# The output stored by GpSimd's indirect transfers, one tile at a time, in place of SyncE's plain ones

## Chip, cores and metric

The kernel runs on one core of one Trainium2 chip. The metric is the device time in microseconds of one execution. Engines are named as in the profile: PE (TensorE), DVE (VectorE), ACT (ScalarE), POOL (GpSimd), SP (SyncE).

## What is computed

Four transformer layers in sequence, each a cross-attention and a feed-forward part, on x of 16 x 256 rows of 128 float32 values (4096 rows) with a context of 16 x 64 rows. The parts are called a0, f0, a1, f1, a2, f2, a3, f3. The last, f3, is a mixture of 8 experts of which the best two count for each row, with 2 shared experts that always count:

```python
p = softmax(h @ gate_w.T)                        # h: x normalised
gate = where(p + gate_bias >= second largest, p, 0)
x = x + sum(gate[e] * (silu(h @ w1[e].T) * (h @ w3[e].T)) @ w2[e].T for e in range(8))
x = x + (silu(h @ sw1.T) * (h @ sw3.T)) @ sw2.T
```

The output is x after f3, 4096 rows of 128 float32, 2.1 MB.

## The kernel before

The state stays on the chip for the whole program, in the buffer X of 128 partitions by 32 tiles by 128 values: row 128 t + p of the output is partition p of tile t. The work goes by groups of four tiles (GT = 4), 8 groups (N_GROUPS), in every part. All engines run their own program and wait for each other by semaphores.

In f3 each group goes through 10 chunks (CH3): 8 experts and 2 halves of the shared one. For a chunk PE makes two products of the turned rows with the weights (L2199 and L2202), ACT applies silu to the first (L2249), DVE multiplies with the second (L2270), and PE makes the product back to 128 columns (L2216 for experts, L2219 for the shared halves). DVE adds each expert's product, weighted by its gate, to X, tile by tile (L2279). After the last chunk DVE has, in this order: the gates of the next group (L2160 to L2181), the normalised rows of the group after it (L271), and the add of the shared part, L2297, which is the last write to a group's four tiles of X. It waits for that write and raises the semaphore `sem("f3", "res")` by one. So the result of a group is announced after L2297; DVE goes on with L2270 of the next group.

SP issues all loads at the start (L2357 to L2373; only the weights of f3 wait for space). Then it loops over the groups: it waits for a group's result (L2375), and stores the four tiles in one transfer of 256 KB (L2376), 512 pieces of 512 bytes. After the loop it waits until the eight have landed (`S("stored")`).

POOL, in f0, takes part in a reduction across partitions (L1174). In the attention parts it makes products for the values (L422) and adds bias rows to X (L415); in f2 it has most of its work (L1951, L1961). Its last work is that of attention a3, `heads_pool(pool, heads["a3"])`, the last call in its program. It has none in f3.

PE's program has its next groups' turned rows prepared ahead; the order of all engines in f3 is written out by hand.

Of the kernel before, what the change touches and what calls it, by code (L numbers as in the profile page):

```python
# [19 lines left out]
U8 = mybir.dt.uint8  # L20
I16 = mybir.dt.int16
U16 = mybir.dt.uint16
ALU = mybir.AluOpType
ACT = mybir.ActivationFunctionType
AX = mybir.AxisListType
ds = bass.ds

P = 128
B, SQ, SK, D = 16, 256, 64, 128
N_TILES = B * SQ // P  # L30
N_GROUPS = N_TILES // 4
GT = 4
# [39 lines left out]
def build(nc, dram):  # L72
    with ExitStack() as ctx:
        def sb(name, shape, dt=F32):
            return ctx.enter_context(nc.sbuf_tensor(name, shape, dt))
# [3 lines left out]
        def S(name):  # L79
            if name not in sems:  # L80
                sems[name] = ctx.enter_context(nc.semaphore(name))
            return sems[name]

        X = sb("X", [P, N_TILES, D])
# [10 lines left out]
        for k, parts in PACKS.items():  # L96
            pack_sb[k] = shared[k] if k in shared else sb("w_" + k, [P, WIDTH[k]])
            at = 0
# [55 lines left out]
        def groups2(eng, body):  # L154

            with eng.Fori(0, N_GROUPS // 2 - 1) as k:
                for j in range(2):
# [15 lines left out]
                   res=N_GROUPS, bn=N_TILES)  # L173
# [11 lines left out]
        def sem(s, name):  # L185
            return S("all_" + name)

        def at(s, name):
            return sum(count(x, name) for x in SUB[:SUB.index(s)])
# [18 lines left out]
        def ln_var_dve(dve, s, k=0):  # L208
# [7 lines left out]
            dve.wait_ge(sem(s, "stats"), at(s, "stats") + k + 1)  # L216
            dve.tensor_tensor(diff, me, mo, ALU.subtract).then_inc(ln, 1)
            dve.scalar_tensor_tensor(out=var, in0=ve, scalar=D * LN_EPS, in1=vo, op0=ALU.add, op1=ALU.add).then_inc(ln, 1)
            dve.tensor_tensor(mn, me, mo, ALU.add).then_inc(ln, 1)
            dve.wait_ge(ln, n + 1)  # L220
            dve.scalar_tensor_tensor(out=sq, in0=diff, scalar=0.25, in1=diff, op0=ALU.mult, op1=ALU.mult).then_inc(ln, 1)
            dve.wait_ge(ln, n + 3)
            dve.tensor_scalar(mn, mn, 0.5, None, ALU.mult).then_inc(ln, 1)
            dve.wait_ge(ln, n + 4)
            dve.scalar_tensor_tensor(out=var, in0=var, scalar=1.0 / D, in1=sq, op0=ALU.mult, op1=ALU.add)\
                .then_inc(sem(s, "var"), 1)
# [123 lines left out]
        def hs(name):  # L350
            return S("att_" + name)

        def hat(s, name):
            rotated = 2 if s == "a3" and name == "k_ps" else 0
            return ATT_A0.get(name, 0) + HSUB.index(s) * PER[name] + rotated
# [49 lines left out]
        def heads_pool(pool, L):  # L405
            s = L.s
            pool.wait_ge(S("rows"), 1)
            row = addrow[:, HAS_ROW[s], :]
            if s == "a3":
                pool.wait_ge(S("f2_tr"), 4 * N_GROUPS)  # L410

            def rows(g):
                pool.wait_ge(sem(s, "normed"), at(s, "normed") + g + 1)
                xg = X[:, ds(4 * g, 4), :]
                pool.tensor_tensor(xg, xg, row.unsqueeze(1).to_broadcast([P, GT, P]), ALU.add)\  # L415
                    .then_inc(sem(s, "biased"), 1)

            def weights(b):
                pool.wait_ge(hs("v"), hat(s, "v") + b // 4 + 1)
                if b >= 2:  # L420
                    pool.wait_ge(hs("pv"), hat(s, "pv") + b - 1)
                pool.tensor_tensor(  # L422
                    L.vw[b % 2].rearrange("p (q e n) -> p q e n", q=4, e=2),
                    tile_of(L.V2, b).rearrange("p (q n) -> p q n", q=4).unsqueeze(2).to_broadcast([P, 4, 2, 32]),
                    W["vmask8"].rearrange("p (e n) -> p e n", e=2).unsqueeze(1).to_broadcast([P, 4, 2, 32]),
                    ALU.mult).then_inc(hs("kv"), 1)

            def rotate(b):
                pool.wait_ge(S("att_qe"), b + 1)
                pool.tensor_tensor(L.qe[b % 2], L.qe[b % 2], W["cosq"], ALU.mult).then_inc(hs("r"), 1)  # L430
                pool.tensor_tensor(L.qse[b % 2], L.qse[b % 2], W["sinq"], ALU.mult).then_inc(hs("r"), 1)
                if b >= L.ahead:
                    pool.wait_ge(hs("st_ps"), hat(s, "st_ps") + b - L.ahead + 1)
                pool.wait_ge(hs("r"), 2 * b + 2)
                pool.tensor_tensor(L.qT[b % L.ahead], L.qe[b % 2], L.qse[b % 2], ALU.add).then_inc(hs("qT"), 1)

            if L.rope:
                rotate(0)
                rotate(1)
                weights(0)  # L440
                rotate(2)
                weights(1)
                rotate(3)
                rows(0)
                for b in range(B):
                    if b + 4 < B:
                        rotate(b + 4)
                    if b + 2 < B:
                        weights(b + 2)
                    if b % 2 and b // 2 + 1 < N_GROUPS:  # L450
                        rows(b // 2 + 1)
            else:
                for g in range(N_GROUPS):
                    weights(2 * g)
                    weights(2 * g + 1)
                    rows(g)
# [729 lines left out]
        gate_l = [levels(0), levels(1)]  # L1186
        sig_l = [levels(2, U16), levels(3, U16)]
        sig_f = [tmp_all[:, 2 * F0N + i * F0N:3 * F0N + i * F0N] for i in range(2)]
# [935 lines left out]
        f3 = Carve()  # L2124
# [177 lines left out]
            groups2(dve, body)  # L2302

        def setup_dve(dve):
            dve.wait_ge(S("ld_const"), 16)
            dve.memset(qs[:, 14:32], 0.0).then_inc(S("cst"), 1)
            dve.memset(qs[:, 13:14], ROUND).then_inc(S("cst"), 1)
            dve.tensor_copy(ident16[:, :], ident).then_inc(S("cst"), 1)
            dve.wait_ge(S("ld_x"), 16)  # L2310
            for t in range(LN0):
                dve.bn_stats(stats[:, t, :], X[:, t, :]).then_inc(S("bn0"), 1)
            dve.wait_ge(S("bn0"), LN0)
            dve.sem_inc(sem("a0", "stats"), 1)
# [39 lines left out]
        @block.sync  # L2354
        def _(sp):
            x_in = dram["x"].rearrange("(t p) d -> p t d", p=P)
            sp.dma_start(X[:, 0:LN0, :], x_in[:, 0:LN0, :]).then_inc(S("ld_x"), 16)  # L2357
            sp.dma_start(pack_sb["const"][:, :], dram["pack_const"]).then_inc(S("ld_const"), 16)
            sp.dma_start(pack_sb["a0"][:, :], dram["pack_a0"]).then_inc(S("ld_a0"), 16)
            sp.dma_start(ctx_sb[:, :, :].rearrange("p b k -> p (b k)"), dram["ctx"]).then_inc(S("ld_ctx"), 16)  # L2360
            sp.dma_start(mask_u8[:, :], dram["mask"]).then_inc(S("ld_mask"), 16)
            sp.dma_start(X[:, LN0:N_TILES, :], x_in[:, LN0:N_TILES, :]).then_inc(S("ld_x"), 16)
            sp.dma_start(kmrow_u8[:, :], dram["kmrow"].to_broadcast([P, B * SK])).then_inc(S("ld_kmask"), 16)
            sp.dma_start(kmT_u8[:, :], dram["kmT"]).then_inc(S("ld_kmask"), 16)
            sp.dma_start(pack_sb["f0"][:, :], dram["pack_f0"]).then_inc(S("ld_f0"), 16)
            sp.dma_start(rows_bc[:, :], dram["rows"].to_broadcast([P, 4 * P])).then_inc(S("ld_rows"), 16)
            sp.dma_start(gbias3[:, :], dram["gbias"].to_broadcast([P, E3])).then_inc(S("ld_rows"), 16)
            sp.dma_start(rscale[:, :], dram["rscale"].to_broadcast([P, 1])).then_inc(S("ld_rows"), 16)
            sp.dma_start(pack_sb["once"][:, :], dram["pack_once"]).then_inc(S("ld_once"), 16)
            for k in ("a1", "f1", "a2", "f2", "a3", "f3"):  # L2370
                if k == "f3":
                    sp.wait_ge(S("f0_o_ps"), N_GROUPS)
                sp.dma_start(pack_sb[k][:, :], dram["pack_" + k]).then_inc(S("ld_" + k), 16)  # L2373
            with sp.Fori(0, N_GROUPS) as g:
                sp.wait_ge(sem("f3", "res"), at("f3", "res") + g + 1 + 1)  # L2375
                sp.dma_start(dram["out"].rearrange("(g t p) d -> p g t d", p=P, t=GT)[:, ds(g, 1)]  # L2376
                             .rearrange("p a t d -> p (a t) d"), X[:, ds(4 * g, 4), :]).then_inc(S("stored"), 16)
            sp.wait_ge(S("stored"), 16 * N_GROUPS)

        @block.vector  # L2380
        def _(dve):
# [45 lines left out]
        @block.gpsimd  # L2427
        def _(pool):
            pool.wait_ge(S("ld_const"), 16)
            att0_pool(pool)  # L2430
            f0_pool(pool)
            heads_pool(pool, heads["a1"])
            heads_pool(pool, heads["a2"])
            f2_pool(pool)
            heads_pool(pool, heads["a3"])

def constants():
# [100 lines left out]
```

## Time and profile before

| | us |
|---|---|
| median of 3 runs | 1238.36 |
| lowest and highest run | 1228.98, 1240.29 |
| the profiled execution, by the same clock | 1236.59 |
| its span, from the first instruction to the last | 1234.8 |

The profile's page tells the busy time of each engine as a share of the span. The table of stretches tells the same for parts of it. A timeline lists instructions in order of time, merged where several of one line follow each other; behind each, in brackets, stands how long its engine sat idle before it and what it was released by. Transfers are issued by a queue (SPq); the time of an issue is not that of the transfer, which is told apart as time to landing. TensorE's granted clock is a share of full speed (2.4 GHz).

### The profile page before, as it was taken

What the parts mean: (1) busy time and instruction counts of PE and PEld (TensorE: products, weight loads), DVE (VectorE), ACT (ScalarE), POOL (GpSimd) and SP (SyncE); (2) the same over time, 40 slices, a digit from 0 to 9 for tenths busy, and PEclk for the clock granted to TensorE, in tenths of its full rate; (3) what the DMA queues carried; (4) which work ended last, traced back from release to release, by engine and by line L of the source; (5) the groups of instructions that cost most, each with busy time, mean ns of one, the idle gap of its engine ahead of it and who ended that gap; (6) DMA issues with size and microseconds to landing.
All of it is one profiled execution on the core that took longest, in us unless ns stands there. A gap on an engine that the chain in (4) does not pass through costs nothing.

```text
span 1234.8 us, 21182 instructions
## 1 busy us (share of the span) xinstructions
PE 1019.8 (83%) x7331; PEld 656.3 (53%) x7331; DVE 906.6 (73%) x2297; ACT 634.7 (51%) x1007; POOL 354.4 (29%) x334
## 2 busy tenths in 40 slices
PE   5868800679978997899669999998889979999998
PEld 3653300655546674454326667666645546666665
DVE  4685699858885674577678898999568876666666
ACT  3424578856632244565267777775466533333332
POOL 5600000002110003345098999995112200000000
PEclk9988965779999997999759999999989999999999
DMA  7000000010000000000000000000000000000000
GB/s 272 1 1 1 1 0 0 1 65 2 1 2 1 1 1 1 2 1 2 1 0 1 1 0 0 0 1 1 1 1 2 2 1 10 9 8 8 8 9 18
DMA packets 8959, 13.51 MB, mean 11 GB/s; under 512 B 816, under 2 KB 6704, under 8 KB 8624
## 3 DMA queue, kind: packets, MB, share of 16 engines
q1 hardware_dynamic: 8880, 12.46, 2.9%
q8 instruction: 50, 0.82, 0.3%
q14 instruction: 29, 0.24, 0.1%
HBM read 10.36 MB, written 2.10 MB: 10 GB/s over the span
## 4 chain that ended last, share of the span: by engine, by line
PE 43%; DVE 26%; issue 7%; ACT 4%; DVEq 0%; ACTq 0%
DVE big L785 7%; DVE hq L780 7%; PE psum L558 5%; PE psum L2216 5%; PE psum L2199 5%; PE psum L2202 5%; PE psum L1518 2%; DVE big L2041 2%; PE psum L1762 2%; PE psum L1770 2%; PE psum L512 2%; DVE big L789 2%; ACT psum L1879 2%; PE psum L1777 2%; PE psum L1773 2%
## 5 line engine op out<-in xcount | busy, mean ns | idle before, releaser
L780 DVE TENSOR_REDUCE hq<-psum 128x16 f32<-128x1024 f32 x96 | 114.3, 1221 | 82.7 <-PE psum L512 42.8
L1951 POOL TENSOR_TENSOR big<-big 128x512 f32<-128x512 f32 x128 | 128.6, 1043 | 21.4 <-ACT big L1856 21.4
L2249 ACT ACTIVATE big<-psum 128x512 f32<-128x512 f32 x80 | 47.7, 598 | 141.1 <-PE psum L2199 141.0
L422 POOL TENSOR_TENSOR big<-big,w_const 128x256 f32<-128x256 f32 x48 | 35.8, 748 | 260.3 <-PE psum L558 227.3
L1879 ACT ACTIVATE psum<-big,tmp 128x512 f32<-128x512 f32 x128 | 85.0, 687 | 25.0 <-DVE big L2041 22.3
L2041 DVE SCALAR_TENSOR_TENSOR big<-big,tmp,psum 128x512 f32<-128x512 f32 x128 | 90.4, 744 | 4.8 <-ACT psum L1879 1.9
L2270 DVE TENSOR_TENSOR big<-big,psum 128x512 f32<-128x512 f32 x80 | 54.4, 687 | 51.1 <-PE psum L2202 49.7
L668 ACT ACTIVATE big<-psum 128x1024 f32<-128x1024 f32 x64 | 62.0, 1021 | 55.1 <-PE psum L542 55.1
L785 DVE RECIPROCAL big<-psum 128x256 f32<-128x256 f32 x48 | 84.0, 1750 | 7.7 <-PE psum L558 7.6
L2216 PEld LDWEIGHTS psum<-tmp,big 128*128 128x128 f32 x512 | 66.7, 192 | 41.5 <-issue 38.0
L2279 DVE SCALAR_TENSOR_TENSOR X<-psum,big,X 128x128 f32 (+1 forms) x256 | 72.3, 344 | 17.9 <-PE psum L2216 15.5
L2202 PE MATMUL psum<-hT,tmp 128*128 128x512 f32 x160 | 81.8, 593 | 2.7 <-DVEq L2260 2.7
L1961 POOL TENSOR_TENSOR big<-big 128x1024 f32<-128x1024 f32 x32 | 75.2, 2360 | 26.3 <-DVE big L2041 26.3
L2199 PE MATMUL psum<-hT,tmp 128*128 128x512 f32 x160 | 82.5, 597 | 0.0
L1432 PE MATMUL psum<-f_downT,tmp 128*128 128x128 f32 x192 | 25.8, 301 | 68.0 <-DVE tmp L1315 68.0
L287 ACT ACTIVATE hT<-psum 128x512 f32<-128x512 f32 x64 | 38.1, 595 | 76.8 <-PE psum L282 76.8
L558 PE MATMUL psum<-big 128*32 128x256 f32 x768 | 53.1, 393 | 28.2 <-DVE big L789 28.2
L2216 PE MATMUL psum<-tmp,big 128*128 128x128 f32 x512 | 68.2, 276 | 8.5 <-DVE big L2270 8.5
L1201 DVE TENSOR_REDUCE amax<-big 128x1 f32<-128x1536 f32 x32 | 55.9, 1749 | 22.6 <-ACT big L1341 22.6
L282 PE MATMUL psum<-w_const,hrow 128*128 128x128 f32 x256 | 44.4, 301 | 33.8 <-DVE hrow L1225 10.9
L538 PE MATMUL psum<-hq,big 32*128 32x256 f32 x768 | 65.6, 428 | 6.9 <-DVE hq L780 6.6
L1801 PEld LDWEIGHTS psum<-w_const,big 128*128 128x128 f32 x512 | 61.0, 192 | 8.6 <-issue 8.6
(243 smaller groups left out, 2353.5 us busy)
## 6 DMA issues: line engine op xcount, KB each, us to landing
out<-X SPq DMA_DIRECT2D x8, 256.0 KB, 2.3
tmp<-in_pack_f SPq DMA_DIRECT2D x1, 1924.0 KB, 7.4
w_f<-in_pack_f SPq DMA_DIRECT2D x1, 1280.0 KB, 12.2
tmp<-in_pack_once SPq DMA_DIRECT2D x1, 960.0 KB, 7.1
X<-in_x SPq DMA_DIRECT2D x1, 768.0 KB, 5.3
w_a<-in_pack_a SPq DMA_DIRECT2D x3, 256.0 KB, 7.5
w_a<-in_pack_a SPq DMA_DIRECT2D x1, 704.0 KB, 9.6
w_f<-in_pack_f SPq DMA_DIRECT2D x1, 576.0 KB, 5.0
```

The costliest lines, as they stand in the source:

```text
L538: pe.matmul(bank(1 + r)[:, 256 * e:256 * e + 256], L.kbd[rows, b, e * P:(e + 1) * P], L.qT[b % L.ahead][rows, :], start=True, stop=False)
L558: ins = pe.matmul(bank(6)[32 * r:32 * r + 32, 256 * which:256 * which + 256], w, L.pt[b % 2][:, (2 * r + e) * 256:(2 * r + e + 1) * 256], ...
L780: dve.tensor_reduce(nm, psum[:, 1 + 2 * t:3 + 2 * t, :].rearrange("p c (r l k) -> p (c r) l k", r=2, k=SK), AX.X, ALU.max, negate=True).th ...
L785: dve.reciprocal(L.rz, bank(6)[:, 256:512]).then_inc(hs("rz"), 1)
L1879: act.activation(bank(EX_BANK + h % 2), ssum[t][:, h * 512:(h + 1) * 512], ACT.Exp, bias=shift2[:, t * NH2 + h:t * NH2 + h + 1]).then_inc( ...
L1951: ins = pool.tensor_tensor(ssum[t][:, h * 512:(h + 1) * 512].rearrange("p (i j) -> p i j", i=ROWS2), st[:, 0, h, 0:ROWS2].unsqueeze(2).to_ ...
L1961: pool.tensor_tensor(ew[t][:, 0:left], ew[t][:, 0:left], ew[t][:, NFOLD * 512:], ALU.add)\
L2041: dve.scalar_tensor_tensor(out=ew[t][:, blk], in0=ssum[t][:, blk], scalar=best2[:, t, h, 7:8], in1=bank(EX_BANK + h % 2), op0=ALU.is_ge, o ...
L2199: pe.matmul(bank(1 + e % 2), W["f3_w1"][:, e * P:(e + 1) * P], hT[:, j, :], start=True, stop=True)\
L2202: pe.matmul(bank(3 + e % 2), W["f3_w3"][:, e * P:(e + 1) * P], hT[:, j, :], start=True, stop=True)\
L2216: ins = pe.matmul(bk[:, t * P:(t + 1) * P], hid3[e % 2][:, t * P:(t + 1) * P], W["f3_w2"][:, e * P:(e + 1) * P], start=True, stop=True) \
L2279: dve.scalar_tensor_tensor(out=xt, in0=bank(5 + e % 2)[:, t * P:(t + 1) * P], scalar=gate3[:, t * E3 + e:t * E3 + e + 1], in1=xt, op0=ALU. ...
```

## The change

SP's loop over the groups, with its eight stores and the wait for them, is taken out. POOL gets a new function, `store_pool`, called behind `heads_pool(pool, heads["a3"])`. It writes a table of row numbers once: `tok_row[p, t] = 128 t + p`, 128 partitions by 32 unsigned integers. Then, for each group, it waits for the same semaphore value as SP did, and issues four indirect transfers, one for each tile: each takes its 128 row numbers from a column of the table and writes 128 rows of 512 bytes to the output. There are 32 in all, of 64 KB. At the end POOL waits for all of them. No other engine's program is changed.

```diff
@@ -2302,6 +2303,19 @@
             groups2(dve, body)
 
 
+        tok_row = sb("tok_row", [P, N_TILES], U32)
+
+        def store_pool(pool):
+
+            pool.iota(tok_row[:, :], [[P, N_TILES]], base=0, channel_multiplier=1).then_inc(S("tok_row"), 1)
+            pool.wait_ge(S("tok_row"), 1)
+            for g in range(N_GROUPS):
+                pool.wait_ge(sem("f3", "res"), at("f3", "res") + g + 1 + 1)
+                for t in range(4 * g, 4 * g + 4):
+                    pool.indirect_dma_start(dram["out"], bass.IndirectOffsetOnAxis(tok_row[:, t:t + 1], 0),
+                                            X[:, t, :], None).then_inc(S("stored"), 16)
+            pool.wait_ge(S("stored"), 16 * N_TILES)
+
         def setup_dve(dve):
             dve.wait_ge(S("ld_const"), 16)
             dve.memset(qs[:, 14:32], 0.0).then_inc(S("cst"), 1)
@@ -2371,11 +2385,6 @@
                 if k == "f3":
                     sp.wait_ge(S("f0_o_ps"), N_GROUPS)
                 sp.dma_start(pack_sb[k][:, :], dram["pack_" + k]).then_inc(S("ld_" + k), 16)
-            with sp.Fori(0, N_GROUPS) as g:
-                sp.wait_ge(sem("f3", "res"), at("f3", "res") + g + 1 + 1)
-                sp.dma_start(dram["out"].rearrange("(g t p) d -> p g t d", p=P, t=GT)[:, ds(g, 1)]
-                             .rearrange("p a t d -> p (a t) d"), X[:, ds(4 * g, 4), :]).then_inc(S("stored"), 16)
-            sp.wait_ge(S("stored"), 16 * N_GROUPS)
 
         @block.vector
         def _(dve):
@@ -2433,6 +2442,7 @@
             heads_pool(pool, heads["a2"])
             f2_pool(pool)
             heads_pool(pool, heads["a3"])
+            store_pool(pool)
```

## Rows read from the trace of the kernel before

**Rows 1.** The page: busy us (share of the span) xinstructions; the chain that ended last.

```profile
PE 1019.8 (83%) x7331; PEld 656.3 (53%) x7331; DVE 906.6 (73%) x2297; ACT 634.7 (51%) x1007; POOL 354.4 (29%) x334
...
PE 43%; DVE 26%; issue 7%; ACT 4%; DVEq 0%; ACTq 0%
```

**Rows 2.** Stretches of f3: length; busy us (xinstructions) by engine; clock, DMA share, GB/s.

```profile
1007.00:1033.00 26.00, 26.00 (x124) 16.68 (x122) 17.63 (x57) 9.09 (x14) 0.00 (x0) 1.00 0.00 1
...
1158.00:1182.00 24.00, 22.87 (x110) 14.72 (x109) 15.98 (x51) 8.17 (x12) 0.00 (x0) 1.00 0.04 11
...
1207.00:1232.00 25.00, 24.13 (x115) 15.45 (x113) 16.56 (x43) 5.38 (x9) 0.00 (x0) 1.00 0.04 11
```

**Rows 3.** Timeline of one expert in the last group: start us, us, instruction.

```profile
1220.28 1.02 PE L2202 MATMUL psum<-hT,tmp 128*128 128x512 f32 x2
...
1221.40 0.69 DVE L2270 TENSOR_TENSOR big<-big,psum 128x512 f32<-128x512 f32 x1 [0.65 <-PE psum L2202]
...
1222.23 1.13 DVE L2279 SCALAR_TENSOR_TENSOR X<-psum,big,X 128x128 f32<-128x128 f32 x4
...
1222.89 1.02 PE L2202 MATMUL psum<-hT,tmp 128*128 128x512 f32 x2
```

**Rows 4.** Timeline of the border between the first two groups of f3.

```profile
1031.70 1.16 DVE L271 TENSOR_SCALAR hrow<-X,lnw 128x128 f32 x4 [0.39 <-DVE big L2181]
...
1032.77 0.68 DVE L2297 TENSOR_TENSOR X<-X,psum 128x512 f32 x1
...
1033.78 1.28 DVE L2270 TENSOR_TENSOR big<-big,psum 128x512 f32<-128x512 f32 x2 [0.32 <-PE psum L2202]
...
1034.60 1.15 PE L2216 MATMUL psum<-tmp,big 128*128 128x128 f32 x8 [1.09 <-DVE big L2270]
```

**Rows 5.** Timeline of the last stores, and the end's instructions (duration ns, first and last start).

```profile
1207.02 25.47 SPq L2376 DMA_DIRECT2D out<-X  x2
...
1231.17 0.69 DVE L2297 TENSOR_TENSOR X<-X,psum 128x512 f32<-128x512 f32 x1 [1.25 <-PE psum L2219]
1232.11 0.38 SPq L2376 DMA_DIRECT2D out<-X  x1
...
L73 SPq COMPARE_BRANCH  x1: 38/38/38, 1234.4 to 1234.4; - x1
...
L73 PEldq EVENT_SEMAPHORE  x1: 51/51/51, 1234.8 to 1234.8; - x1
```

**Rows 6.** The stores' line: duration ns min/median/max, first and last start; time to landing.

```profile
L2376 SPq DMA_DIRECT2D out<-X x8: 378/378/415, 1033.7 to 1232.1; - x8
...
DMA to landing us min/median/max: 2.3/2.3/2.4
```

**Rows 7.** Waits of SP's queue: us in total, times, longest us.

```profile
SPq L2376 <- DVEq L2300: 969.5, 8, 777.5
...
SPq L73 <- DMA out<-X: 1.8, 1, 1.8
```

**Rows 8.** POOL's own lines: duration ns min/median/max, and its last work.

```profile
L422 POOL TENSOR_TENSOR big<-big,w_const x48: 722/725/1707, 229.2 to 986.5; 128x256 f32<-128x256 f32 x48
...
L415 POOL TENSOR_TENSOR X<-X,addrow x24: 1261/1266/1278, 246.3 to 987.2; 128x512 f32<-128x512 f32 x24
...
L1961 POOL TENSOR_TENSOR big<-big x32: 2342/2360/2375, 635.4 to 854.6; 128x1024 f32<-128x1024 f32 x32
...
987.17 1.26 POOL L415 TENSOR_TENSOR X<-X,addrow 128x512 f32<-128x512 f32 x1
```

**Rows 9.** POOL after its last reduction across partitions: timeline, and the queue's change.

```profile
221.69 0.37 POOL L1174 PARTITION_ALL_REDUCE qs<-qs  x1 [29.20 <-DVEq L1154]
229.18 1.42 POOL L422 TENSOR_TENSOR big<-big,w_const 128x256 f32<-128x256 f32 x2 [7.13 <-issue]
...
L422 POOLq MODIFY_POOL_CONFIG  x2: 85/85/85, 222.0 to 222.0; - x2
```

**Rows 10.** Timeline of SP's queue in the loads at the start: start us, us.

```profile
3.62 0.86 SPq L2362 DMA_DIRECT2D X<-in_x  x1
4.52 5.25 SPq L2363 DMA_DIRECT2D kmrow_u<-in_kmrow  x1
9.81 0.43 SPq L2364 DMA_DIRECT2D kmT_u<-in_kmT  x1
```

**Rows 11.** GB/s moved in 40 slices of 1230 to 1236 us.

```profile
GB/s 0 0 0 0 0 0 0 0 0 0 0 0 0 0 0 0 0 0 0 0 171 304 300 283 287 287 116 0 0 0 0 0 0 0 0 0 0 0 0 0
```

**Rows 12.** DVE's lines beside POOL's work and without it: duration ns min/median/max.

```profile
L2041 DVE SCALAR_TENSOR_TENSOR big<-big,tmp,psum x128: 735/743/750, 632.4 to 853.8; 128x512 f32<-128x512 f32 x128
...
L2270 DVE TENSOR_TENSOR big<-big,psum x80: 678/687/689, 1004.9 to 1229.2; 128x512 f32<-128x512 f32 x80
```

More of the change, by code:

```diff
@@ L22 @@
 U16 = mybir.dt.uint16
+U32 = mybir.dt.uint32
 ALU = mybir.AluOpType
```

## The prediction

> **What bounds the kernel now.** I read the page first for the shares of the engines [rows 1]. PE is busy for 83% of the span, DVE for 73%, POOL for 29%, and the chain that ended last is PE, then DVE. No share of it is a transfer. The change touches only the last stage, f3, so I then took the table by stretches of 24 to 26 us there [rows 2]. PE is busy for 23 to 26 us of each at full granted clock, DVE for 16 to 18, ACT for at most 9, and POOL does nothing: its column is empty from 1007 us on. The stage runs at the pace of PE. The reader is to see there that the engine that gets the new work is idle, and that the stores move only some 10 GB/s.
>
> Next I followed one expert in order of time [rows 3]. It repeats every 2.61 us (1220.28 to 1222.89), and DVE works 0.69 + 1.13 = 1.82 us of it, so DVE has 0.8 us to spare per expert. A group border is tighter [rows 4]: PE waits 1.09 us for the product of L2270 after the residual add L2297, and that row is the one place where a DVE delay reaches PE at once.
>
> Last I read the end [rows 5]. The last add, L2297, starts at 1231.17 and takes 0.69, so it ends at 1231.86. SP issues its last store at 1232.11, 0.25 us later. The store lands a median 2.3 us after its issue [rows 6], at 1234.4, where SP's last branch stands, and the last event is at 1234.8. **The tail that depends on how the output is written is thus 1234.8 - 1231.9 = 2.9 us**; all stores but the last land under the matmuls of a later group. The waits on SP's own queue say the same: it stood 969.5 us waiting for DVE in 8 waits, and 1.8 us waiting for a transfer, once [rows 7]. SP is never late.
>
> **The change, part by part.**
>
> *Removed:* eight issues of 256 KB on SP, 0.38 us each [rows 6]. Seven lie under PE's work and give back nothing. The eighth is in the tail. Its 2.3 us to landing is 0.38 of issue and 1.9 after it.
>
> *Added, the iota and its wait:* one 128x32 write on POOL. The nearest row is a 128x256 tensor operation on POOL at 0.72 us [rows 8]. POOL is free from 987.17 + 1.26 = 988.4 us, and the first group is ready only at 1033.7 [rows 6]. It costs nothing, with 45 us of cover; without that cover, under 1 us. POOL may also have to change its configuration for a kind of instruction that it has not run before. The trace shows one such change: after the fourth cross-partition reduction the next product, L422, starts 7.1 us late, with a change of POOL's configuration at its head and nothing else to wait for [rows 9]. Such a 7.1 us lies in the same 45, or, if it comes with the first scatter, under the 198 us between the first group and the last (1232.1 - 1033.7). In the tail it would cost 7.1 in full, but all scatters are of one kind, so it is over by then.
>
> *Moved:* the wait for a group's result goes from SP to POOL. It is moved past POOL's work of the attention stages, which is over at 988.4. Behind it on POOL stand only the later scatters and the last wait, and no engine waits for a semaphore of POOL in f3. On SP nothing is left behind the weight loads. The groups follow each other by (1232.1 - 1033.7) / 7 = 28.3 us on average, and the last two by 25.1 (the seventh store starts at 1207.0 [rows 5]). Four scatters fit in that as long as one takes less than 6.3 us. So 28 of the 32 scatters are hidden, and the last four are not.
>
> *Added, the last four scatters.* Each is an instruction on POOL that has to work out where 128 rows of 512 B go, 64 KB in all. The trace has no indirect transfer, and no transfer of POOL's. Call its time on POOL c. From below the nearest row is an SP issue, 0.38 us [rows 6], that is 1.5 us for four. From above it is POOL's slowest operation, 2.36 us (L1961) [rows 8], 9.4 for four; the slowest issue of a transfer on any queue is that of the mask row, 5.25 us [rows 10], 21 for four. I take the middle row of POOL, the 1.27 us of L415 [rows 8], because an instruction that handles each of 128 rows in software-like steps should cost more than the issue that SP makes in 0.38, and nothing in it touches as many elements as L1961 does. The four go one after another: 4 x 1.27 = 5.1 us. Then the last one has to land. I take the 1.9 us that the SP store needs after its issue. It may be 0.6 less, because only 64 KB are left and not 256 (the last store moved at close to 300 GB/s [rows 11], so 192 KB less is 0.6 us). The end after the landing stays 0.4 us.
>
> The sum, for the last group: 4c + 1.9 in place of 2.3, that is an addition of **4c - 0.4 us**. With c = 1.27 it is 5.1 - 0.4 = 4.7; with 0.38, 1.1 (0.5 with the faster landing); with 2.36, 9.0; with 5.25, 20.6. The profiled span becomes 1234.8 + 4.7 = 1239.5. That execution took 1236.59 us by the clock of the runs, which is 1.8 below the median of 1238.36, so on the median I forecast 1238.36 + 4.7 = **1243.1 us**.
>
> *What the transfers meet.* The 16 engines of DMA are idle in f3 but for the stores (a share of at most 0.04 in [rows 2]). Four transfers of 64 KB in place of one of 256 KB change nothing that anybody waits for before the end.
>
> *A rule that speaks against the change.* The last store's whole time to landing is 2.3 us in this trace, from SP [rows 6]. The Trainium skill (DMA: Bandwidth & Descriptors, Anatomy of one DMA — SWDGE (gpsimd) path) says that a transfer issued by GpSimd has a fixed cost of about 2.0 us plus its bytes by 436 GB/s, most of it the receipt from the memory written, and that descriptor generation is small. By that, an estimate from that page, four scatters overlap but for the issue and end 2.15 us after the last issue: an addition below mine. If they didn't overlap, four times 2.15 us would be 8.6, an addition of 6.3. Neither leaves 1%. No row here shows a transfer issued by POOL.
>
> **The rivals.** About 1% (12.4 us) is what a measurement of this kernel can tell from no change: its three runs alone spread over 11.3 us.
>
> *A. The tail grows by a few microseconds, the rest stays.* For it: POOL is empty, PE is the pace, the other 28 scatters have cover. Time 1239.5 to 1250, likeliest 1243. It holds for c up to 3.2 us, from 4c - 0.4 = 12.4.
>
> *B. One scatter costs much more than any operation of POOL here.* Its place is the same tail. It decides from c = 3.2 us. With c like the 5.25 of the mask row it gives 1238.4 + 20.6 = 1259. From 6.3 us on, the scatters of one group don't end before the next group, and the lateness adds up to the end. For it: that one SP issue [rows 10] shows that the making of a transfer can take that long. Against it: its neighbours take 0.86 and 0.43, and what it does, one short row into 128 partitions, is not what a scatter does.
>
> *C. POOL's work slows DVE at the borders of the groups.* The scatters of a group start right as DVE starts L2270 after L2297, and there PE already waits 1.09 us for DVE [rows 4]. If DVE stood still for all 5.1 us of each batch, at 7 borders, that would be 36 us, and 1243 + 36 = 1279. DVE gets back 0.8 us per expert, but PE has then already waited. It decides from (12.4 - 4.7) / 7 = 1.1 us lost per border. Against it: POOL writes little when it prepares a transfer. Where both worked at once in an earlier stage (L1961 from 635.4 to 854.6 in [rows 8]), this trace shows no cost to L2041, whose 128 rows keep between 735 and 750 ns for 128x512 beside 687 ns for L2270 without POOL [rows 12], at most 63 ns on each, and that is another operation. The Trainium skill (SBUF — State Buffer, Who interferes with whom) says that the two exclude each other where DVE runs in a 2-port mode or reads two inputs from SBUF. By that rule only L271, a tensor with scalars, could meet it, and at a border it ends before the result is announced; L2270 reads one input from PSUM. So by the rule C doesn't happen.
>
> *D. Nothing changes.* With c at 0.38 and the faster landing the addition is 0.5 us, 1239. The change does what it says, so the stores are certain to move; but the most that any other way to write the output could win is the 2.9 us of the tail, 0.2%. Faster by over 1% has no mechanism in this profile; I leave it only what the spread of the runs (1228.98 to 1240.29) could make.
>
> **How the numbers follow.** A 0.70, D 0.14, B 0.08, C 0.05, and 0.03 for a faster result from the spread alone. The time is that of A, 1243. The range: low 1233, which is D less the 6 us by which a median of this kernel may fall lower (its lowest run is 9.4 under the median). High 1256, which takes B in up to c = 4.5 us (4 x 4.5 - 0.4 = 17.6 above 1238.4) and leaves out its rest and C. Out of the range are then about 0.05 of C, 0.05 of B and 0.06 on either side for spread. Faster 0.03, within 1% 0.84 (A and D), slower 0.13 (B and C).
>
> **What the profile of the changed kernel would show.** POOL has 32 transfers in f3, in batches of four, each batch 25 us or more after the last one, and the time of one is c. The last L2297 still ends at about 1232 less or more the spread; from there to the end it is 7.6 us in place of 2.9. PE's wait at a border for L2270 stays near 1.1 us, which tells A from C. If the last scatter starts over 10 us after the last add, B is right. The prediction is wrong if c is above 3.2 us, if the transfers of one batch wait for each other's landing for more than 2 us each, if the end of the program after the last landing is no longer 0.4 us, or if L2270, or four of L2279, take longer than 0.69 and 1.13 us behind a batch.

## The result, and the profile after

The changed kernel takes 1244.62 us (median of 14 runs, 1236.90 to 1246.07), the kernel before 1238.14 (14 runs). The ratio is 1.0051 with a 95% interval of 1.0039 to 1.0063, that is 6.3 us more by the ratio (4.8 to 7.8): within 1%, and not zero. The profiled execution took 1244.06 us with a span of 1242.2. Lines of kernel.py are shifted: L2297 of before is L2298 now, L2270 is L2271, L2279 is L2280, L2216 is L2217, and the instructions that close the program, L73, are L74.

The page of the changed kernel (busy us, share of the span, instructions; the new line of POOL; the queue of POOL's transfers with packets, MB and share of 16 engines):

```profile
PE 1019.9 (82%) x7331; PEld 655.7 (53%) x7331; DVE 905.9 (73%) x2297; ACT 634.5 (51%) x1007; POOL 385.5 (31%) x367
...
q0 software_dynamic: 1024, 2.10, 0.5%
...
L2315 POOL DMA_INDIRECT out<-X,tok_row x32 | 31.0, 968 | 217.4 <-DVEq L2301 210.1
```

Against [rows 1] PE, DVE and ACT are unchanged. POOL has 31.1 us more work, and 31.0 of it are the 32 scatters. The span is 7.4 us longer, so the difference is a wait somewhere, and the end shows where. This is the timeline of the last 11 us, POOL and DVE among it:

```profile
1232.11 0.69 DVE L2298 TENSOR_TENSOR X<-X,psum 128x512 f32<-128x512 f32 x1 [1.25 <-PE psum L2220]
1233.13 0.95 POOL L2315 DMA_INDIRECT out<-X,tok_row  x1 [20.35 <-DVEq L2301]
1234.39 0.95 POOL L2315 DMA_INDIRECT out<-X,tok_row  x1 [0.30 <-issue]
1235.65 0.96 POOL L2315 DMA_INDIRECT out<-X,tok_row  x1 [0.30 <-issue]
1236.91 0.96 POOL L2315 DMA_INDIRECT out<-X,tok_row  x1 [0.30 <-issue]
```

and these are the instructions that close the program on POOL's queue and the last one of PE's (duration ns min/median/max, first and last start us), with the landing time of the scatters (its maximum of 3.3 belongs to the seventh group, not to the last).
```profile
DMA to landing us min/median/max: 2.2/2.2/3.3
```

```profile
L74 POOLq COMPARE_BRANCH  x1: 41/41/41, 1239.2 to 1239.2; - x1
L74 POOLq DRAIN  x1: 2682/2682/2682, 1239.3 to 1239.3; - x1
...
L74 PEldq EVENT_SEMAPHORE  x1: 51/51/51, 1242.2 to 1242.2; - x1
```

The last add ends at 1232.80. From there to the end it is now 9.4 us, where [rows 5] gave 2.9. The reader sees three pieces: 0.33 us until POOL starts and four scatters that start 1.26 us apart, to 1237.87; 1.3 us until the last one has landed, at 1239.2, where POOL's branch behind the wait stands; and then a DRAIN of POOL's queue that takes 2.68 us, so that 3.0 us pass from that branch to the end. In the kernel before, 0.4 us passed between SP's branch behind its wait and the end [rows 5]. The difference of the two tails, 9.4 - 2.9 = 6.5 us, is the whole of the measured 6.3. The last add itself ended 0.94 us later than in the kernel before (1232.80 and 1231.86). That is no effect of the stores: POOL's last addition, L416, ahead of all scatters, was already 0.97 us late (988.14, beside 987.17 in [rows 8]), and experiments 1 and 2 settle it.

At the borders of the groups nothing changed. The timeline of the first border, beside [rows 4]:

```profile
1033.72 0.68 DVE L2298 TENSOR_TENSOR X<-X,psum 128x512 f32 x1
1034.72 1.28 DVE L2271 TENSOR_TENSOR big<-big,psum 128x512 f32<-128x512 f32 x2 [0.32 <-PE psum L2203]
...
1035.55 1.15 PE L2217 MATMUL psum<-tmp,big 128*128 128x128 f32 x8 [1.09 <-DVE big L2271]
```

PE waits the same 1.09 us. The other borders agree: over all of f3, PE's waits for this product sum to 8.5 us in 7 times before and 8.4 us in 7 times after (the last column of the two pages):

```profile
L2216 PE MATMUL psum<-tmp,big 128*128 128x128 f32 x512 | 68.2, 276 | 8.5 <-DVE big L2270 8.5
...
L2217 PE MATMUL psum<-tmp,big 128*128 128x128 f32 x512 | 68.2, 276 | 8.4 <-DVE big L2271 8.4
```

All 80 of L2271 keep to the durations of [rows 12] within 1 ns, and here are also the 256 of L2280, after and before (there L2279):

```profile
L2271 DVE TENSOR_TENSOR big<-big,psum x80: 679/687/690, 1005.8 to 1230.2; 128x512 f32<-128x512 f32 x80
```

```profile
L2280 DVE SCALAR_TENSOR_TENSOR X<-psum,big,X x256: 339/343/352, 1007.9 to 1229.2; 128x128 f32 x96, 128x128 f32<-128x128 f32 x32
...
L2279 DVE SCALAR_TENSOR_TENSOR X<-psum,big,X x256: 339/343/352, 1006.9 to 1228.2; 128x128 f32 x96, 128x128 f32<-128x128 f32 x32
```

### The profile page after: what moved, and what is told of

Same layout as the page of the kernel before. It is cut to its first block, busy times and chain, and to the rows that moved or that the text cites. A ratio compares the mean times of both kernels' runs of the same rounds, so it can differ in the third digit from the quotient of the medians.

```text
span 1242.2 us, 21165 instructions
## 1 busy us (share of the span) xinstructions
PE 1019.9 (82%) x7331; PEld 655.7 (53%) x7331; DVE 905.9 (73%) x2297; ACT 634.5 (51%) x1007; POOL 385.5 (31%) x367
## 4 chain that ended last, share of the span: by engine, by line
PE 42%; DVE 26%; issue 7%; ACT 4%; DVEq 0%; POOL 0%; ACTq 0%
DVE hq L781 7%; DVE big L786 7%; PE psum L559 5%; PE psum L2217 5%; PE psum L2200 5%; PE psum L2203 5%; PE psum L1519 2%; DVE big L2042 2%; PE psum L1763 2%; PE psum L1771 2%; PE psum L513 2%; DVE big L790 2%; ACT psum L1880 2%; PE psum L1778 2%; PE psum L1774 2%
## 5 line engine op out<-in xcount | busy, mean ns | idle before, releaser
L2315 POOL DMA_INDIRECT out<-X,tok_row x32 | 31.0, 968 | 217.4 <-DVEq L2301 210.1
L2271 DVE TENSOR_TENSOR big<-big,psum 128x512 f32<-128x512 f32 x80 | 54.4, 687 | 51.1 <-PE psum L2203 49.7
L2217 PEld LDWEIGHTS psum<-tmp,big 128*128 128x128 f32 x512 | 66.6, 192 | 41.5 <-issue 38.0
L2280 DVE SCALAR_TENSOR_TENSOR X<-psum,big,X 128x128 f32 (+1 forms) x256 | 72.2, 344 | 18.0 <-PE psum L2217 15.5
L2217 PE MATMUL psum<-tmp,big 128*128 128x128 f32 x512 | 68.2, 276 | 8.4 <-DVE big L2271 8.4
```

What stands on the lines that cost most here:

```text
L2217: ins = pe.matmul(bk[:, t * P:(t + 1) * P], hid3[e % 2][:, t * P:(t + 1) * P], W["f3_w2"][:, e * P:(e + 1) * P], start=True, stop=True) \
L2280: dve.scalar_tensor_tensor(out=xt, in0=bank(5 + e % 2)[:, t * P:(t + 1) * P], scalar=gate3[:, t * E3 + e:t * E3 + e + 1], in1=xt, op0=ALU. ...
```

## The experiments

Ratios are to the kernel before, run on the same chip, with 95% intervals. Since single medians here are good to a few microseconds only, the tail (from the end of the last add to the end of the span in the profiled execution) is the finer measure, and each verdict rests on it first. It is read from one execution of each kernel.

### 1. The last group by SP, the other seven by POOL

```diff
-            for g in range(N_GROUPS):
+            for g in range(N_GROUPS - 1):          # POOL: 28 scatters, then it waits for them
...
+            sp.wait_ge(sem("f3", "res"), at("f3", "res") + 7 + 1 + 1)
+            sp.dma_start(out_of_group_7, X[:, 28:32, :]).then_inc(S("stored_sp"), 16)
+            sp.wait_ge(S("stored_sp"), 16)
```

(Here and below, `out_of_group_7` and the like stand for the output's rows of that group, comments behind # are added for the reader, and lines left out are marked `...` or follow from those shown.)

> Groups 0 to 6 are stored by POOL's 28 scatters, the last group by one plain transfer of SP. Theory (all of the loss lies behind the last add L2298: four scatters one after another, and the 2.7 us DRAIN of POOL's queue behind its last wait): from the end of the last add to the end of the span 2.9 to 3.0 us as in the kernel before, time against the kernel before 0 (within 1 us); POOL's DRAIN runs at about 1215 us, far ahead of the end. Rival (the 28 early scatters or the changed program cost something ahead of the tail; f3 began 0.9 us later in the changed kernel's profiled execution): the time stays 1 us or more above that of the kernel before, though the tail is short.

Measured: 1237.88 us, beside 1237.47 before, ratio 1.0003 (0.9980 to 1.0026). Closing instructions of this kernel (ns, first and last start us):

```profile
L74 POOLq COMPARE_BRANCH  x1: 41/41/41, 1214.2 to 1214.2; - x1
L74 POOLq DRAIN  x1: 2356/2356/2356, 1214.4 to 1214.4; - x1
```

The last add ended at 1232.28 + 0.69 = 1232.97 and the span at 1235.8, a tail of 2.8 us. The DRAIN is there, 18 us ahead of the last add, under PE's work. So 28 of the scatters and the row numbers cost nothing that this comparison can see, and the loss is in the tail. Here too the last add ended 1.1 us later than in the kernel before, with the same time over the runs; in experiment 2, with all 32 scatters, it ended over 1 us earlier (1230.71). So that lateness is what one execution differs from the next. The interval alone would leave the rival up to 3 us; that the two tails differ by 6.5 us and the runs by 6.3 (4.8 to 7.8) leaves it at most 1.3. The DRAIN took 2.36 us and not 2.68, though in both kernels it starts behind the wait for the landing, with nothing in flight; what differs is that 28 transfers were issued and not 32, and that small difference turned out to be the clue.

### 2. The last wait on SP

```diff
-            pool.wait_ge(S("stored"), 16 * N_TILES)
+            sp.wait_ge(S("stored"), 16 * N_TILES)      # in SP's program, behind the loads
```

> All 32 scatters stay on POOL; only the last wait for their landing goes from POOL to SP, so POOL's DRAIN may start 1.3 us earlier, right after the last scatter. Theory (the DRAIN is a fixed 2.7 us of POOL's own, whatever is in flight): it ends 1.3 us earlier, tail 9.4 - 1.3 = 8.1 us. Rival (the DRAIN waits until the transfers have landed and then does its 2.7 us): it gets longer, about 4 us, and the tail stays 9.4.

Measured: 1243.39 us, ratio 1.0049 (1.0026 to 1.0073). POOL's last scatter, and the closing instructions:

```profile
1234.82 0.96 POOL L2315 DMA_INDIRECT out<-X,tok_row  x1 [0.30 <-issue]
```

```profile
L74 POOLq DRAIN  x1: 7658/7658/7658, 1230.8 to 1230.8; - x1
L74 SPq COMPARE_BRANCH  x1: 38/38/38, 1237.1 to 1237.1; - x1
```

The DRAIN now stands in the queue from 1230.8, behind four scatters that end at 1235.78; it ends at 1230.8 + 7.66 = 1238.5, 2.7 us after them. So it doesn't first wait for the landing (which SP saw at 1237.1) and then take its 2.7: the 2.7 run from the last scatter on. Since the landing falls inside them, this run doesn't tell whether a shorter DRAIN would have had to wait for it; the last experiment does. The last add ended at 1230.71, the span at 1238.7: a tail of 8.0 us, as the theory had it (8.1). The time alone wouldn't have told 8.0 from 9.4.

### 3. Half rows, twice the scatters

```diff
+            halves = dram["out"].rearrange("r (h d) -> (r h) d", h=2)
...
+                    for h in range(2):
+                        c = h * N_TILES + t
+                        pool.indirect_dma_start(halves, bass.IndirectOffsetOnAxis(tok_row[:, c:c + 1], 0),
+                                                X[:, t, 64 * h:64 * h + 64], None).then_inc(S("stored"), 16)
```

> Each scatter is cut in two that write 128 half rows of 256 bytes, 64 scatters in all, 8 in the tail; the bytes are the same. Theory (a scatter costs POOL by its count of rows or by being an instruction, 1.26 us each from start to start): tail 9.4 + 4 x 1.26 = 14.4 us, time 5 us over that of the changed kernel, so about 11 over the kernel before. Rival (it costs by bytes): 0.63 each, tail 9.4, no further loss.

Measured: 1249.80 us, ratio 1.0104 (1.0065 to 1.0143). The 64 scatters, and the DRAIN:

```profile
L2320 POOL DMA_INDIRECT out<-X,tok_row x64: 952/958/1306, 1033.4 to 1240.0; - x64
```

```profile
L74 POOLq DRAIN  x1: 5296/5296/5296, 1242.3 to 1242.3; - x1
```

A scatter of half the bytes takes the same 0.958 us, so it costs by the instruction with its 128 rows and not by bytes. No run changed the number of rows, so whether the instruction or its rows set the price is open. But the tail is 1247.9 - 1230.84 = 17.1 us, not 14.4: the DRAIN doubled as well, to 5.30. That contradicted the part of the theory that called it fixed.

### 4. Plain transfers, but from POOL

```diff
-                for t in range(4 * g, 4 * g + 4):
-                    pool.indirect_dma_start(...)
+                pool.dma_start(out_of_group_g, X[:, 4 * g:4 * g + 4, :]).then_inc(S("stored"), 16)
```

> The kernel before with its eight plain transfers of 256 KB issued by POOL in place of SP: no row numbers, no indirect transfers. Theory (the DRAIN belongs to any transfer that POOL makes, the scatters only add their number): one instruction of about 1 us, landing 1.3 to 2 us later, DRAIN 2.7: tail 0.3 + 1 + 1.9 + 2.7 + 0.2 = about 6 us, +3 against the kernel before. Rival (the DRAIN belongs to indirect transfers alone): tail about 3.5 us, +0.6.

Measured: 1238.63 us, ratio 1.0000 (0.9979 to 1.0021). POOL's eight transfers, and the DRAIN:

```profile
L2310 POOL DMA_DIRECT2D out<-X x8: 750/750/1069, 1034.6 to 1232.9; - x8
```

```profile
L74 POOLq DRAIN  x1: 721/721/721, 1235.8 to 1235.8; - x1
```

The tail is 1236.8 - 1232.58 = 4.2 us, 1.3 over the kernel before and too little for the timing. Neither side was right: the DRAIN belongs to plain transfers as well, but it took 0.72 us. These eight transfers write the same 4096 rows as the 32 scatters do, so neither rows nor bytes set the DRAIN; the number of transfers does.

### 5. Only the last group by POOL

```diff
-            for g in range(N_GROUPS):
+            for g in range(N_GROUPS - 1, N_GROUPS):    # POOL: four scatters; SP's loop keeps groups 0 to 6
```

> Groups 0 to 6 are stored by SP as in the kernel before, only the last group by four scatters of POOL. The first scatter of the program is now in the tail. Theory (the DRAIN does not depend on how many scatters there were; the first scatter of a program takes 1.31 us in place of 0.96 and starts 1.0 us after the add in place of 0.33): DRAIN 2.7, tail 9.4 + 0.35 + 0.7 = 10.4 us. Rival 1 (the DRAIN grows with the number of transfers made): under 1 us, tail about 8.5. Rival 2 (the first use costs POOL the 7 us of a change of configuration that the trace of the kernel before shows at L422): tail about 16.

Measured: 1241.58 us, beside 1237.16 before, ratio 1.0034 (1.0012 to 1.0055). The first scatter of this program, and the DRAIN:

```profile
1233.23 1.31 POOL L2315 DMA_INDIRECT out<-X,tok_row  x1 [244.34 <-DVEq L2301]
```

```profile
L74 POOLq DRAIN  x1: 396/396/396, 1239.8 to 1239.8; - x1
```

The tail is 1240.4 - 1232.20 = 8.2 us. My theory (10.4) falls and rival 1 (8.5) holds: with four transfers made, the DRAIN takes 0.40. The first scatter started 1.03 us after the add and took 1.31, so a first use costs 1.05 us over the others (0.7 + 0.35), far from the 7 us of rival 2.

The DRAIN over all kernels so far:

| transfers issued by POOL | 4 | 8 (plain, 256 KB) | 28 | 32 | 64 |
|---|---|---|---|---|---|
| its DRAIN, us | 0.396 | 0.721 | 2.356 | 2.682 | 5.296 |
| 0.07 + 0.0817 for each | 0.397 | 0.724 | 2.358 | 2.684 | 5.299 |

### 6. The kernel before with its last group in two halves

```diff
+                    for h in range(2):                 # DVE, last group: two tiles each
+                        dve.tensor_tensor(xh, xh, bank(5)[...256 h...], ALU.add).then_inc(S("f3_half"), 1)
...
+            for h in range(2):                         # SP
+                sp.wait_ge(S("f3_half"), h + 1)
+                sp.dma_start(two_tiles, X[:, t:t + 2, :]).then_inc(S("stored_h%d" % h), 16)
```

> The kernel before with its last group's add and store cut in two halves on SP, so that only 128 KB are left after the last add. Theory (the tail of the kernel before is mostly fixed latency, only the moving of bytes shrinks): tail 2.9 - 0.4 = 2.5 us; the time does not tell it from the kernel before. Rival (two issues one after another on SP cost as much as the bytes save): tail 2.9 or more.

Measured: 1236.77 us, beside 1237.16, ratio 0.9990 (0.9971 to 1.0009). The tail is 1235.0 - 1232.47 = 2.5 us, as expected. That is the best end found here. It wins 0.4 us of the tail by the profile, which the time doesn't tell from zero.

### 7 and 8. An early drain

```diff
             for g in range(N_GROUPS):
+                if g == N_GROUPS - 1:
+                    pool.drain()
                 pool.wait_ge(sem("f3", "res"), at("f3", "res") + g + 1 + 1)
```

> The changed kernel with one drain instruction more on POOL, ahead of the wait for the last group, so behind 28 scatters; all else as it is. The first six runs gave POOL's DRAIN as 0.07 us + 0.082 us for each transfer that POOL had issued (0.40 with 4, 0.72 with 8, 2.36 with 28, 2.68 with 32, 5.30 with 64), whatever was in flight. Theory (a drain settles the transfers issued so far, once): the early drain takes about 2.4 us under PE's matmuls, the last one only counts four, 0.40; tail 9.4 - 2.3 = 7.1 us. Rival (the count goes over all transfers since the start of the program, at each drain): early 2.4, last 2.68 again, tail 9.4.

Measured: 1241.03 us, beside 1236.71 before, ratio 1.0030 (1.0010 to 1.0051). The two drains of POOL:

```profile
L2314 POOLq DRAIN  x1: 7424/7424/7424, 1210.5 to 1210.5; - x1
```

```profile
L74 POOLq DRAIN  x1: 380/380/380, 1242.0 to 1242.0; - x1
```

The early one stands behind scatters that end at 1215.47, so 1210.5 + 7.42 - 1215.47 = 2.45 us are its own, near the 2.36 with 28 transfers in the table. The last took 0.38, and the tail is 1242.6 - 1235.48 = 7.1 us. A drain settles what was issued since the last one; the rival, which counts from the start of the program, falls.

The last run has the early drain and the wait for the landing on SP (as in experiment 2) together.

> As the last one, and the wait for the landing on SP. Theory (early drain settles 28): POOL's last drain (0.40) lies under the landing, the tail is 0.33 + 3 x 1.26 + 2.2 to landing + 0.4 = 6.7 us, 3.8 over the kernel before, all of it from the number of scatters in a row. Rival (the drain counts all again): tail 8.0 as with the wait on SP alone.

Measured: 1240.15 us, ratio 1.0034 (1.0018 to 1.0049). SP's branch behind its wait, at the landing:

```profile
L74 SPq COMPARE_BRANCH  x1: 38/38/38, 1239.7 to 1239.7; - x1
```

The tail is 1240.1 - 1233.31 = 6.8 us (6.7 expected). POOL's last scatter and the DRAIN behind it:

```profile
1237.43 0.95 POOL L2317 DMA_INDIRECT out<-X,tok_row  x1 [0.30 <-issue]
```

```profile
L74 POOLq DRAIN  x1: 6432/6432/6432, 1233.4 to 1233.4; - x1
```

The DRAIN had four transfers to settle and was expected to take 0.40 us. It ends at 1233.4 + 6.43 = 1239.8, which is 1.5 us after the last scatter's end (1238.38) and 0.2 us after its landing (1239.6). So this DRAIN didn't end before its transfers had landed. In experiment 2 this didn't show, as the 2.7 us for 32 transfers were longer than the 1.3 us to the landing. That the work for each transfer goes on while the last ones are in flight fits both runs; that the DRAIN has to wait for the landing rests on this one run.

With the early drain, 3.9 us over the kernel before are left, and they are the four scatters in a row (5.1 us until the last is issued, where SP needed 0.6) less the shorter landing. By the runs alone the intervals of this kernel (1.0018 to 1.0049), of experiment 7 and of the changed kernel (1.0039 to 1.0063) overlap, so the gain over them is read from the tails.

## Why the prediction was right, and where a term was off

- *Faster, same or slower, and the likeliest case.* Case A came about: 1244.62 measured, 1243 forecast, inside 1233 to 1256 and inside A's 1239.5 to 1250. The addition was 6.3 us by the runs and 6.5 by the tails, where the sum said 4.7. The time alone is weak support for the working: the range would have held anything from no change to 17 us more, and the sum came within 1.8 us of the tails because errors of opposite sign met in it, as the next points show.
- *The tail is all that the way of storing can move.* Shown by experiment 1: with the last group back on SP the ratio is 1.0003, with 28 scatters on POOL ahead of it. The row numbers took 0.16 us on POOL at 989.36, under the cover that was forecast.
- *The price of a scatter, c = 1.27, taken from POOL's L416.* The start-to-start distance is 1.26 us, 0.96 of work and 0.30 until the next starts. The number is right; the reasoning, that it would be like a middle-sized operation of POOL, was a choice between 0.38 and 2.36 and no derivation, so that it hit is luck. Nothing waits for the 0.30 behind the last of the four, so they take 3 x 1.26 + 0.96 = 4.7 us and not 5.1. That the price doesn't go by the bytes was open, and experiment 3 shows it.
- *The landing, 1.9 us after the last issue or 0.6 less.* The 0.6 less was right: 1.3 us (1237.87 to 1239.2). The size of the transfer as its reason is borne out by experiment 4, where 256 KB from POOL landed 2.7 us after the start of their issue, 1.9 to 2.0 after its end.
- *"The end after the landing stays 0.4 us."* This is the term that failed. It is 3.0 us, of which 2.68 are a DRAIN of POOL's queue. The prediction had put it among the signs of being wrong, and the sign came: the tail is 9.4 us where 7.6 was forecast. The trace of before had this instruction on POOL at its end, where POOL had issued no transfer, and I did not ask what it would have to do once POOL had some:

```profile
L73 POOLq DRAIN  x1: 2017/2017/2017, 986.5 to 986.5; - x1
```

It ended at 986.5 + 2.02 = 988.5, about 0.1 us after POOL's last addition (988.43), which fits the table's 0.07 for no transfers. With the right landing the sum would have been 4.1; with the DRAIN it is 4.1 + 2.6 = 6.7, beside 6.5 measured; the 0.2 between them are the 0.3 behind the last scatter, less 0.08 by which POOL starts later after the add than SP did.
- *POOL's change of configuration.* The first scatter did cost more, 1.05 us and not 7.1 (experiment 5), and lay under PE's work as forecast. The trace records no change of configuration at it, so what the 1.05 us are is open.
- *Rival B* decided from c = 3.2 us; c is 1.26. *Rival C* needed 1.1 us lost per border; PE's wait at the first border is 1.09 us before and after, its waits over all borders 8.5 and 8.4, and no row of L2271 or L2280 is longer than before by more than 1 ns at its maximum. The Trainium skill's rule on what excludes DVE and GpSimd (SBUF — State Buffer, Who interferes with whom) agrees with this trace, though weakly: of DVE's instructions only L2271 (20 times) and L2280 (36 times) ran beside a scatter, each reads one of its two tensors from PSUM, so that by the rule neither can meet it, and none became longer than before by more than 1 ns. The prediction named L271 alone as one that could meet the rule; the gates of the next group also read two inputs from SBUF (L2172 for one), but they run some 20 us after a batch of scatters has ended. *Case D* needed an addition of 0.5 us; the interval of 4.8 to 7.8 leaves it out.
- *The rule against the change*, a fixed cost of 2.0 us plus bytes from the Trainium skill (DMA: Bandwidth & Descriptors, Anatomy of one DMA — SWDGE (gpsimd) path): the trace has 2.2 us from the start of a scatter to its landing, beside the rule's 2.15. So the landing came as by the rule. But the scatters of a row follow each other on POOL, each holding it for 0.96 us with 0.30 behind it, and the DRAIN comes after the landing, where the rule's time ends.

What stays open: what the DRAIN does for each transfer. The runs show only that its time goes by their number since the last drain, and, in experiment 8, that it ended only after they had landed. Also open are whether a scatter's price goes by the instruction or by its rows, and whether the 28 hidden scatters cost some tenths of a microsecond ahead of the tail, which lies below what these runs resolve.

## What to carry to other kernels

When an output is stored group by group, only the last group's store is exposed, as long as the others fit between two groups (here 5 us of scatters in 25), so count what stands between the last arithmetic and the last instruction of the program, the closing instructions of each queue among it, and put the fewest and shortest issues there: one plain transfer from SP had 2.9 us, four scatters from POOL 9.4. If scatters from POOL are needed, keep their number down (at 128 rows each, half the bytes cost the same), let another engine wait for the landing, and put a drain of POOL under other work shortly before the end: that brought the tail from 9.4 down to 6.8 us, which the times over the runs are too coarse to confirm.

## What the hardware showed that I had not expected

- The DRAIN of POOL's queue at the end of the program takes 0.07 us plus 0.082 us for each transfer that POOL has issued since the last drain: about 0.1 us with none, 0.40 with 4, 0.72 with 8, 2.36 with 28, 2.68 with 32, 5.30 with 64. Plain transfers of 256 KB count like scatters of 64 or 32 KB. These times are with all of them landed. Right behind the last scatter, the DRAIN ended 2.7 us later with 32 transfers to settle, as without anything in flight, but 1.5 us later with four: 0.2 us after the landing.
- A plain transfer of 256 KB (512 rows) held POOL for 0.75 us, less than a scatter of 128 rows at 0.96; SP's issue of the same took 0.38.
- The first transfer of a program on POOL is dearer: a scatter took 1.31 us in place of 0.96 and started 0.7 us later after its semaphore, a plain one took 1.07 in place of 0.75.
